# Loading each chunk of the next image in two halves, with a semaphore for each half

## The reference

```
x = x + conv_block(_gn(x))                       # _gn: 32 groups of 16 channels, over all pixels
h = relu(bn1(conv1x1(r, conv1_w)))               # r = _gn(x), 512 -> 128 channels
q = bnq(conv1x1(h, q_w)); k = softmax over pixels of conv1x1(h, k_w); v = bnv(conv1x1(h, v_w))
pos = convolution of each channel of v with 16 filters of 15 x 15 (emb)
out = q . (k v^T)  +  q . pos                    # 4 heads, 16 keys, 32 values -> 128 channels
conv_block = relu(bn3(conv1x1(relu(bn2(out)), conv3_w)) + r)
```

## Time and profile before

| | |
|---|---|
| median of 3 runs | 4817.78 us (4816.66 to 4820.35) |
| the profiled execution | 4817.23 us, its span 4815.5 us |
| TensorE busy | 4457.8 us, 93% |
| VectorE, ScalarE, GpSimd busy | 2796.9, 2346.0, 967.9 us (58%, 49%, 20%) |
| mean granted TensorE clock | 0.949 of full speed |
| moved by DMA | 1284.17 MB in 537174 packets, 267 GB/s |
| X loads from SP | 132 of 2048 KB, median 20.1 us from issue to landing |

### The profile page before, as it was taken

The page is one execution under the profiler, slowest core; times in us unless marked ns, Lnnn a source line. Parts: engine busy times, 40 slices in busy tenths (PEclk is TensorE's granted clock), DMA queues, the critical chain, the costliest instruction groups (busy, mean ns, idle before and its releaser), DMA issues.

```text
span 4815.5 us, 121009 instructions
## 1 busy us (share of the span) xinstructions
PE 4457.8 (93%) x49366; PEld 2717.4 (56%) x49366; DVE 2796.9 (58%) x4631; ACT 2346.0 (49%) x2880; POOL 967.9 (20%) x529
## 2 busy tenths in 40 slices
PE   4899999999999999999999999999999999999997
PEld 2555565655556655555555555555565556555555
DVE  3465555565655665656656556556566565566564
ACT  1455445554545454445544454544455444545453
POOL 0022211122201222202222112222122221112221
PEclk9899999999999999999999999999999999999998
DMA  3689778888778897788887788977888878889877
GB/s 96 214 278 308 239 265 279 275 296 277 249 272 266 282 309 250 254 274 288 281 291 243 265 266 276 307 251 254 272 292 281 288 245 275 270 273 305 263 248 250
DMA packets 537174, 1284.17 MB, mean 267 GB/s; under 512 B 43048, under 2 KB 225324, under 8 KB 528556
## 3 DMA queue, kind: packets, MB, share of 16 engines
q1 hardware_dynamic: 471276, 1017.22, 65.7%
q10 hardware_dynamic: 65472, 260.05, 14.7%
HBM read 844.79 MB, written 432.33 MB: 265 GB/s over the span
## 4 chain that ended last, share of the span: by engine, by line
PE 45%; SPq 18%; DMA 13%; issue 11%; DVE 6%; POOL 4%; ACT 2%; ACTq 0%; POOLq 0%; DVEq 0%
PE ring L527 16%; DMA X<-x_dram 11%; PE ring L653 10%; PE ring L508 7%; SPq L402 5%; PE ring L583 4%; SPq L360 4%; DVE st L884 3%; DMA q_parts<-region 3%; SPq L377 3%; POOL X L1189 2%; PE ring L534 2%; POOL region L1182 2%; SPq L378 2%; PE ring L539 2%
## 5 line engine op out<-in xcount | busy, mean ns | idle before, releaser
L702 ACT COPY region<-ring 126x1024 f32<-126x1024 f32 x1120 | 1102.9, 1016 | 948.0 <-PE ring L508 934.0
L583 PE MATMUL ring<-h,w3T 128*128 128x512 f32 x2048 | 937.7, 601 | 28.6 <-DVE X L1038 15.3
L653 PE MATMUL ring<-region,V 126*32 126x128 f32 x24576 | 889.2, 289 | 42.9 <-issue 42.7
L527 PE MATMUL ring<-X,w1e 128*128 128x512 f32 x2048 | 907.7, 596 | 3.2 <-DVE w1e L910 3.2
L508 PE MATMUL ring<-Qt,Ep 96*126 96x256 bf16 x5120 | 808.3, 298 | 103.9 <-DVE region L702 52.0
L653 PEld LDWEIGHTS ring<-region,V 126*32 126x32 f32 x24576 | 692.0, 116 | 223.3 <-issue 206.8
L702 DVE COPY region<-ring 126x1024 f32<-126x1024 f32 x416 | 507.5, 1220 | 496.6 <-PE ring L508 496.5
L508 PEld LDWEIGHTS ring<-Qt,Ep 96*126 96x126 bf16 x5120 | 598.9, 146 | 323.1 <-issue 139.4
L884 DVE BATCH_NORM_STATS2 st<-X 128x6 f32<-128x512 f32 x1024 | 624.8, 679 | 198.0 <-DMA X<-x_dram 197.9
L527 PEld LDWEIGHTS ring<-X,w1e 128*128 128x128 f32 x2048 | 384.5, 190 | 468.8 <-issue 465.5
L583 PEld LDWEIGHTS ring<-h,w3T 128*128 128x128 f32 x2048 | 370.0, 190 | 410.9 <-issue 371.5
(11 more groups left out here) (130 smaller groups left out, 3317.4 us busy)
## 6 DMA issues: line engine op xcount, KB each, us to landing
X<-x_dram SPq DMA_DIRECT2D x132, 2048.0 KB, 20.1
out_dram<-X SPq DMA_DIRECT2D x512, 512.0 KB, 8.0
X<-x_dram ACTq DMA_DIRECT2D x124, 2048.0 KB, 10.6
Qt<-q_parts SPq DMA_DIRECT2D x768, 128.0 KB, 3.1
V<-v_windows SPq DMA_DIRECT2D x96, 1024.0 KB, 10.5
lambda_sums<-S SPq DMA_DIRECT2D x64, 1024.0 KB, 5.0
h<-lambda_sums SPq DMA_DIRECT2D x256, 256.0 KB, 5.0
q_parts<-region SPq DMA_DIRECT2D x128, 256.0 KB, 4.2
```

The lines of the kernel that those rows point to most:

```text
L527: last = nc.tensor.matmul(dst[:, hh * HALF:(hh + 1) * HALF], w1e[:, c, :], X[:, j, c, hh * HALF:(hh + 1) * HALF], start=(c == 0), stop=(c ...
L583: last = nc.tensor.matmul(dst[:, yb * HALF:(yb + 1) * HALF], w3T[:, t, :], src, start=True, stop=True)
L653: last = nc.tensor.matmul(bank_of(i)[c * DV:(c + 1) * DV, (g % 4) * P:(g % 4 + 1) * P], V[0:TROWS, VSLOT[t], xb, yb * DV:(yb + 1) * DV], W ...
L702: return engine_copy(dst, src)
```

## The change

Each chunk of the next x is loaded by two DMAs of 512 columns in place of one of 1024. Each half has a semaphore of its own. The statistics wait at the first operation of each half, and TensorE's "c0" waits for all eight halves. The reload for the residual and the tail's `reload` stay whole. The bytes moved, the operations on them and their order stay.

```diff
-        x_in = [sem(f"x_in{j}") for j in range(NCH)]
+        x_in = [[sem(f"x_in{j}{hh}") for hh in range(2)] for j in range(NCH)]
...
             def load_x(im, j):
-                sp.dma_start(X[:, j, :, :], xv[im, :, :, j * CHUNK:(j + 1) * CHUNK]).then_inc(x_in[j], 16)
+                for hh in range(2):
+                    sp.dma_start(X[:, j, :, hh * HALF:(hh + 1) * HALF],
+                                 xv[im, :, :, j * CHUNK + hh * HALF:j * CHUNK + (hh + 1) * HALF]).then_inc(x_in[j][hh], 16)
...
                     for i in range(NCH):
-                        pe.wait_ge(x_in[i], im * 16 + 16)
+                        for hh in range(2):
+                            pe.wait_ge(x_in[i][hh], im * 16 + 16)
...
                 j, hh, c = n // 8, n // 4 % 2, n % 4
-                if n % 8 == 0:
-                    dve.wait_ge(x_in[j], im * 16 + 16)
+                if c == 0:
+                    dve.wait_ge(x_in[j][hh], im * 16 + 16)
```

## The result

The changed kernel took 4832.93 us (median of 8 runs, 4822.76 to 4851.65) beside 4819.07 us for the kernel before (8 runs, 4805.13 to 4829.13). The ratio is **1.0034, 95% interval 1.0018 to 1.0050**: slower by 0.34%, some 16 us (the two medians lie 14 us apart). The forecast was 4796 us, range 4774 to 4824. The profiled execution took 4837.9 us, 5 us over its median; its span is 4836.2 us, against 4815.5 before.

The account below looks back on a forecast made before the run. TensorE was taken as the bound, with 40.4 us of pauses hanging on the landing of x. Savings of 29.4 and 11.0 us, less 3.6, 12.5 and 2.4, gave -21.9 us: 4796 us, range 4774 to 4824.

Parts of the forecast that it names:

- What bounds it: TensorE, busy nearly all the time; 40.4 us (0.84%) of its pauses for VectorE hang on the landing of x.
- steps 1 and 3: Landing of x: ordered halves end three statistics 2.5 us earlier; then ScalarE's pause gives back 12.5 us.
- the next limit: TensorE at L508 waits 0.48 us for ScalarE once VectorE is on time, in 26 of 31 images: 12.5 us.
- Step 2: X loads: a 2 KB row costs 89 ns, a chunk takes 5.7 us, and 3.6 us of pauses remain.
- the start: VectorE's first setup operation waits for parameters issued behind the X loads: 2.4 us more, once.
- The queue's share: X loads' DMA queue over the whole run: expected to grow by 1.5 to 2 points.
- Sum: Whole run: - 29.4 + 3.6 - 11.0 + 12.5 + 2.4 = -21.9 us, 4796 us on the median.
- rival B: TensorE: half or more of the gain turns into longer "issue" pauses, 4808 to 4822 us; chance 0.28.
- Its sign of being wrong: TensorE: the forecast is wrong if "issue" pauses grow by as much as VectorE's shrink.
- Rival C: X loads: 2 KB rows are dear, so slower, 4865 us at 119 ns a row; chance 0.14.
- T + 5.1: Landing of chunk 1 in the kernel before, 5.1 us after chunk 0; the first half was forecast 1.6 us sooner.
- Step 4: Work queued behind the X loads: added waits cost nothing; SP's issue ends 2.4 us later, plus up to 2, hidden.

Follow-up runs that it names:

- e1: The changed kernel's two DMAs a chunk with 2 KB rows, but statistics wait for both halves: 4831.96 us beside 4807.48 us before, ratio 1.0050.
- e9: e2 with the statistics in their old order and waiting for both halves of a chunk: 4815.78 us beside 4817.70 us before, ratio 0.9996.
- e4: Kernel before, but loop loads bring 64 KB of each 2 MB chunk (probe, mostly stale x): 4674.36 us beside 4813.65 us, ratio 0.9709.
- e3: Kernel before with whole-chunk loads, weight piece (3, 3) given from VectorE to ScalarE: 4805.68 us beside 4807.48 us, ratio 0.9989.
- e2: The changed kernel with halves cut by channel tiles (4 KB rows), statistics tile by tile: 4801.83 us beside 4807.48 us before, ratio 0.9985.
- e5: Kernel before with each chunk in four DMAs of 1 KB rows, statistics waiting for all four: 4894.72 us beside 4813.65 us, ratio 1.0161.

## Why the prediction was wrong, point by point

- **What bounds it, and steps 1 and 3: right as far as they go.** The halves land in order, VectorE's pauses in `lam` went from 40.0 to 0.8 us, and the next limit took 11.8 us of it (forecast 12.5). But of the "issue" pauses it weighed only the 42.7 us at L653; in `lam` they are 107.7 us.
- **Step 2, price of a row: right in size, wrong in what it was multiplied with.** Forecast 89 ns, measured 84. A chunk takes 5.4 us instead of 5.7. But I charged the longer full stretch only to VectorE's landing (3.6 us) and the start (2.4, measured 3.5). Its effect on TensorE itself had no term: e1 against e9 puts the rows at 26 us in all. The queue's share grew by 0.8 points, not by 1.5 to 2, as two rows cost 9 ns more than one of 4 KB and not 19.
- **Sum, the missing term: this is the step that failed.** I put the change of the issue pauses and of TensorE's own work at nothing, unless rival B came true. They measured +25.5 and +15.9 us in `lam`. e4 shows that these pauses hang on the load of the DMA engines, and e3 that taking 31 us of VectorE's pauses away adds 11 to 21 us of them; the traces show that they end with the instruction queue's packets, and that the longer ones are followed by a lower clock. So early landing brings 6 us (e2, 0.15%), not 28, and with 26 us for the rows 20 us slower is to be expected; 16 were measured by the ratio. By ratios, 0.9985 x 1.0054 = 1.0039, within the interval of 1.0034.
- **Rival B** named the mechanism, "half or more of the gain turns into a longer wait", and underrated it: it had no price for the longer full stretch, so its times ended at 4822. Its sign of being wrong, that the issue pauses grow by as much as VectorE's shrink, came true by two thirds (25.5 of 39.2 us).
- **Rival C** had the right sign for a wrong reason. Its condition, a first half of chunk 1 later than T + 5.1, did not come true.
- **Step 4: right.** SP's two V loads end at 2099.8, 26.5 us after the X issue began and not 24.3, and nothing waits for them. That rows and not DMAs hold SP back is borne out: the X issue takes 12.0 us in the median image before, 15.0 with twice the DMAs (e9) and 20.1 with twice the rows too. Passed waits cost nothing that can be measured (e9).
- The advice of the Trainium skill for larger transfers (Perfetto Trace Analysis, DMA Optimizations) was right in sign. The page's "Batching multiple small transfers into larger ones (e.g., 2KB → 4KB or 8KB)" fits the runs if it is read of rows: two rows of 2 KB cost 2 x 84 = 168 ns of an engine where one of 4 KB cost 159, and the kernel paid 26 us. Two DMAs of 1 MB with the rows left at 4 KB cost nothing that can be measured (e9), and with early landing were 0.15% faster (e2), though the DMA engines were full and not idle.

Of the 26 us of the rows, e1's trace shows 10 us more issue pauses than e9's, 3 us at the start, and 16 us as slower work of TensorE in `lam`, less 3 us of shorter waits for VectorE. The lost clock in `lam` is 22 us more in e1 than in e9, which at the 0.73 to 0.78 us of work that go with a us of it in these two traces is the 16. These are single traces. What stays open is why shorter rows make the packet late, and why a TensorE that is ready sooner does not bring it sooner.

## What to carry to other kernels

When the DMA engines are full, a pause named "issue" inside a run of the same matmuls is a suspect for the instruction queue: look for its packets before counting a saved wait as saved time. A wait removed in front of such a place can come back as another. And a split transfer should keep its row length: cut by channel tile and not by columns, the early landing stayed and the kernel was 0.15% faster than before (e2) instead of 0.34% slower.

## What the runs showed of the hardware that I had not expected

- TensorE's issue pauses depend on what else the DMA engines move: 107.7 us in `lam` with the next x loaded, 43.2 us with 3% of it. The Trainium skill (Runtime: NRT & Kernel Launch, Instruction fetch mechanics) describes the fetch in blocks of 16 KiB through a DMA queue and calls the crossing of a block mostly hidden. The packets of the instruction queue agree (6.82 MB in 416, 16.4 KB each); that the crossing is hidden does not hold here: all 939 issue pauses of over 0.5 us in `lam` end 2.2 to 3.4 us after such a packet has started, at places that lie 123 to 126 matmuls apart.
- A pause of 2.37 us was followed by a granted clock of 0.93 over 2 us and 0.50 over the next 2 us. Over the 20 images of the changed kernel with a pause of more than 1.4 us at this place 1.5 us of clock are lost in the 8 us behind it, so such a pause costs more than its length.
- Rows landing on 128 partitions at full share: 4 KB 411 GB/s, 2 KB 385, 1 KB 349 (e5).
